# A fused attention and fp8 linear kernel: the weights prepared in the order of their use, one scale for each

## The reference

```
xn  = layernorm(x)                               # x: 8 x 2048 x 512, float32, no gain or bias
qkv = xn @ Wqkv.T + bqkv                         # 512 -> 1536
q, k, v in 16 heads of 32; attention runs over the FIRST axis (8 positions), for each of the 2048 columns
mask: rows 0-3 see keys 0-3 only (prompt groups of 4), rows 4-7 see all 8 keys
out = x + softmax(q k / sqrt(32) + mask) v @ Wproj.T + bproj
        + fp8(xn) @ fp8(Wffn).T + bffn           # the same xn; both operands rounded to fp8
```

## Time and profile before

| | |
|---|---|
| time, median of 3 | 1569.23 us (1569.12 to 1570.31) |
| the profiled execution | 1569.3 us, its span 1567.5 us |
| PE busy | 1506.4 us, 96% of the span, 6913 matmuls |
| DVE | 1442.0 us, 92% |
| POOL | 1378.9 us, 88% |
| ACT | 1048.3 us, 67% |
| mean granted TensorE clock | 0.982 |

### The profile page before, as it was taken

The page is one execution under the profiler, slowest core; times in us unless marked ns, Lnnn a source line. Parts: engine busy times, 40 slices in busy tenths (PEclk is TensorE's granted clock), DMA queues, the critical chain, the costliest instruction groups (busy, mean ns, idle before and its releaser), DMA issues. The chain is left out here.

```text
span 1567.5 us, 23119 instructions
## 1 busy us (share of the span) xinstructions
PE 1506.4 (96%) x6913; PEld 681.0 (43%) x6913; DVE 1442.0 (92%) x1188; ACT 1048.3 (67%) x2010; POOL 1378.9 (88%) x1046
## 2 busy tenths in 40 slices
PE   4999999999999999999999999999999999999956
PEld 3444444444444444444444444444444444444412
DVE  7389999999999999999999999999999999999992
ACT  5676667676766767666776776676776667776432
POOL 1288999899899989999998999999899999999885
PEclk8999999999999999999999999999999999999977
DMA  5334454545455454544545455454544445454322
GB/s 197 76 89 113 113 124 118 128 113 128 118 121 121 116 132 106 132 116 125 123 109 134 111 127 122 119 124 111 134 112 128 119 116 128 113 131 97 91 78 81
DMA packets 366508, 184.00 MB, mean 117 GB/s; under 512 B 314160, under 2 KB 314160, under 8 KB 366384
## 3 DMA queue, kind: packets, MB, share of 16 engines
q1 hardware_dynamic: 366384, 182.53, 47.5%
HBM read 73.41 MB, written 33.55 MB: 68 GB/s over the span
## 5 line engine op out<-in xcount | busy, mean ns | idle before, releaser
L391 POOL TENSOR_TENSOR prod_pv<-kv,probs 128x2048 f32<-128x2048 f32 x192 | 699.3, 3642 | 10.0
L758 DVE TENSOR_REDUCE o_nat<-prod_pv 128x512 f32<-128x2048 f32 (+1 forms) x128 | 429.1, 3352 | 51.7 <-POOL prod_pv L391 34.9
L725 DVE TENSOR_REDUCE scores<-prod_qk 128x64 f32<-128x2048 f32 x192 | 439.3, 2288 | 6.6
L720 DVE TENSOR_TENSOR prod_qk<-q_ps,kv 128x1536 f32<-128x1536 f32 (+1 forms) x192 | 397.8, 2072 | 2.2 <-ACT kv L557 2.2
L602 PE MATMUL proj_ps<-wproj_hi,oT 128*128 128x512 f16 x1032 | 339.2, 390 | 0.0
L602 PE MATMUL k_ps<-wqkv_hi,xT 128*128 128x512 f16 x1024 | 327.0, 381 | 5.4 <-DMA xT<-x 5.1
L602 PE MATMUL v_ps<-wqkv_hi,xT 128*128 128x512 f16 x1024 | 325.4, 379 | 0.0
L602 PE MATMUL q_ps<-wqkv_hi,xT 128*128 128x512 f16 x1024 | 325.4, 379 | 0.0
L566 ACT ACTIVATE kv<-v_ps 128x512 f32<-128x512 f32 x128 | 142.3, 1112 | 156.3 <-PE v_ps L602 156.2
L602 PE MATMUL proj_ps<-wproj_lo,oT 128*128 128x512 f16 x516 | 202.1, 392 | 0.0
L602 PE MATMUL k_ps<-wqkv_lo,xT 128*128 128x512 f16 x512 | 195.1, 381 | 0.0
(11 more groups left out here) (117 smaller groups left out, 1853.4 us busy)
## 6 DMA issues: line engine op xcount, KB each, us to landing
xn<-in_L_attn_x SPq DMA_DIRECT2D x128, 256.0 KB, 2.8
xs<-in_L_attn_x SPq DMA_DIRECT2D x128, 256.0 KB, 2.6
out<-xs SPq DMA_DIRECT2D x128, 256.0 KB, 2.1
xT<-x SPq DMA_TRANSPOSE x256, 3.0
kv<-in_L_attn_Wqkv SPq DMA_DIRECT2D x3, 1024.0 KB, 10.4
oT<-o SPq DMA_TRANSPOSE x128, 3.2
kv<-in_L_ffn_weight SPq DMA_DIRECT2D x1, 1024.0 KB, 5.6
kv<-in_L_attn_Wproj SPq DMA_DIRECT2D x1, 1024.0 KB, 14.3
```

What stands on the lines that cost most here:

```text
L391: nc.gpsimd.tensor_tensor(o, v, p, ALU.mult).then_inc(pv_multiplied, 1)
L720: nc.vector.tensor_tensor(prod_qk[:, 1:1 + m0 + 4 - m1, :], qb, k, ALU.mult).then_inc(qk_multiplied, 1)
L725: nc.vector.tensor_reduce(scores[:, n % 2, :, m0:m0 + 4].rearrange("p h m -> p m h"), prod_qk[:, row:row + 4, :].rearrange("p m (h d) -> p ...
L758: nc.vector.tensor_reduce(o_nat[:, n % 2, :], prod_pv[:, place:place + units, :].rearrange("p q (c m) -> p c q m", m=4), AX_XY, ALU.add).t ...
```

## The change

Every weight gets a scale of its own (keys, values, queries, projection, in this order), so that the keys' can be used before the others are loaded. On POOL there are four `partition_all_reduce` of one column in place of one of two columns. SP loads two tiles of x first, then the keys' weight, and the fp8 weight last. The prologue's steps are moved into the slots of each engine. The weights' natural copies move to other parts of `kv`, `prod_pv` and `prod_qk`, since they live longer. Cut to its core:

```diff
 SP, ahead of the slots
-load Wffn; load keys', values', queries' weight; load Wproj; bqkv; k_bias; q_bias; v_bias; bproj; bffn
+            load_x(0, 0)
+            load_x(0, 1)
+            sp.dma_start(wqk_nat[:, 0:KC], ...)            # keys
+            ... bqkv; load_x(0, 2); values; k_bias; queries; q_bias; load_x(0, 3)
+            ... Wproj; v_bias; bproj; bffn; Wffn
 POOL
+            def largest(what):
+                pool.wait_ge(amax_parts, what + 1)
+                nc.gpsimd.partition_all_reduce(amax[:, what:what + 1], amax_part[:, what:what + 1], P, ...)
             def slot(i, j):
-                if at(i, j, L_SOFT):
+                if at(i, j, L_KV):
+                    largest(KEYS)
+                    scale_bias(k_bias, bk_loaded, KEYS, k_bias_ready)
+                    largest(VALUES)
+                if at(i, j, L_KV + 1):
+                    largest(QUERIES)
+                    scale_bias(q_bias, bq_loaded, QUERIES, q_bias_ready)
+                if at(i, j, 7):
+                    largest(PROJ)
+                if at(i, j, 9):
+                    scale_out_biases()
+                if at(i, j, 11):
                     pool.wait_ge(out_bias_summed, 1)
                     split_into_rows(bo_all, out_bias_rows)
+                    pool.wait_ge(small_ready, 2)
+                if at(i, j, 13):
+                    pool.wait_ge(wffn_transposed, KC)
 ACT (high_parts now waits for scales_ready of its weight)
+ slot 4, first: high_parts(0, 4); before the keys' copy: preset_k(), high_parts(4, 8);
+                before the values' copy: high_parts(8, 12)
+ slot 5: the three diagonals; preset_q(0) waits for q_bias_ready
+ slots 7, 8: high_parts(12, 14), (14, 16); 9, 10: q_small, q_half_small; 12, 13: keep_wffn
 PE
+            turn_parts(0, 2 * KC + 2)                       # 10 parts ahead of the slots
+ slot 4: wait for w_ready 4, open k_ps; keys of tile 0; turn_parts(10, 12); wait for w_ready 8,
+         open q_ps 0 and 1; values of tile 0
+ slot 5: wait for w_ready 12 before queries; slot 6: open q_ps 2 and 3
+ slots 7, 8: turn_parts(12, 14), (14, 16)
+ slot 10: the values' bias projected (slot 5 before); slots 11, 12: turn_wffn (24 matmuls each)
+ slot 14: open proj_ps
 DVE
+                if at(i, j, 3):
+                    largest_of_rows(KEYS)
+                if at(i, j, 4):
+                    scale_of(KEYS)
+                    largest_of_rows(VALUES)
+                    low_parts(0, KC)
+                if at(i, j, 5):
+                    scale_of(VALUES)
+                    largest_of_rows(QUERIES)
+                    low_parts(KC, 2 * KC)
+                    scale_of(QUERIES)
+                    low_parts(2 * KC, 3 * KC)
+                if at(i, j, 6):
+                    largest_of_rows(PROJ)
+ slot 7: scale_of(PROJ), low_parts(12, 14), clip and halve Wffn; 8: low_parts(14, 16)
+ slot 9: split the values' bias; slot 10: wait for its projection, add the output biases
```

## The result

The changed kernel takes 1591.88 us (median of four runs, 1590.62 to 1592.41) against 1569.31 for the kernel before on the same chip: 1.0142 times as long, 95% interval 1.0129 to 1.0154. The run profiled took 1592.07 us with a span of 1590.3, against 1567.5: the spans differ by 22.8 us, the medians by 22.6.

A forecast was written before the change was run, and what follows sets the result against it. PE's stream was taken to set the time from the first key product, with DVE a second limit from 100 to 160 us; 1569.3 + 18.3 (DVE's lateness) = 1587.6, said as 1588 us; range 1565 to 1597, the forecast's own 1580 to 1597.

The forecast's parts named there:

- The price of the reductions: On POOL, four reductions between ordinary instructions mean eight changes of code, each taken at 6.5 or 7.03 us.
- the unseen change *into* a reduction: On POOL, code must also be brought in ahead of a reduction; bounds 0 and 7.03 us, hidden before by an 18.05 us wait.
- the first pair: POOL's changes into and out of the keys' reduction, taken at 7.03 us each; the weights' loads may have stretched the one seen.
- the six later ones: POOL's changes of code around the values', queries' and projection's reductions, estimated at 6.5 us each.
- D: Rival: all eight changes at 7.03 us or more, PE at low clock after gaps: 1591 to 1597; chance 0.70 together with the forecast.
- Tile 0's keys: On PE, the first key products start at 25.9 us, 13.4 us earlier; transposes land no earlier than about 25.9.
- The wait in slot 10: DVE waits some 5 us for the projected values' bias before tile 2's scores; 15.9 us from PE's slot 10 to tile 4.
- this chain alone decides: DVE's chain reaches tile 4's slot at 114.3 us against 96.01, 18.3 us late, and sets the end.
- POOL's split of the bias in slot 11: POOL's 6.4 us split moves to slot 11, leaving tile 8's transposes about 4 us early; counted at nothing.
- Rival A: The change of code into the reduction, or the later changes, are free on POOL: 2.3 us won, 1567 us; chance 0.14.
- B: Rival: POOL's changes of code at half the price, 3.6 us each: about 1576 us; chance 0.10.
- C: Rival: as Rival A, and the transposes overtake the weights; keys of tile 0 at 20, 1561 us; chance 0.06.

The follow-up runs named there:

- e1: Changed kernel with each of POOL's four partition reductions replaced by a copy of the one column, the maximum over partitions left out: 1568.28 us, ratio 0.9996.
- e9: Changed kernel with the last-needed loads (projection's and fp8 weight, values' and output biases) issued behind tile 1's transposes: 1590.27 us, ratio 1.0138.
- e4: Changed kernel with DVE's wait for the values' bias and its addition moved to the end of slot 10, behind tile 2's scores: 1590.59 us, ratio 1.014.
- e10: e5 and e9 together, with the queries' maximum transposed only behind tile 0's keys so the keys' bank opens early: 1565.62 us, ratio 0.9979.
- e5: Changed kernel with the maxima made exactly by DVE and a PE transpose, not POOL's reductions; queries' scale and some weight parts reordered: 1570.21 us, ratio 1.0008.
- e11: e10 with DVE's addition of the output biases moved behind tile 2's scores, as in e4: 1564.67 us, ratio 0.9975.
- e2: Changed kernel with all four maxima in DVE's slot 3 and one POOL reduction of four columns in slot 4: 1573.7 us, ratio 1.0031.
- e3: Kernel before with one more POOL partition reduction at the head of slot 7, its result unused: 1576.76 us, ratio 1.005.
- e7: Changed kernel, POOL's four reductions kept, with the last-needed loads issued behind tile 0's transposes: 1592.5 us, ratio 1.0147.
- e6: e5 with the last-needed loads (projection's and fp8 weight, biases) issued behind tile 0's transposes, not ahead of them: 1570.28 us, ratio 1.001.

## Why the prediction was right, and where it was off

**The price of the reductions** was the forecast's whole case, and it holds: e1 takes them away and 23.6 us with them. The forecast's 1588 is 3.9 us short of the 1591.9 measured. The guess that the unseen change *into* a reduction also costs something, with nothing in the trace but a wait in front of it, is right: 5.85 to 8.71 us. The Trainium skill (GPSIMD Engine Reference, "2.1 Instruction dispatch") gives 5.95 us for first-called code; the trace agrees for the three later ways in (5.85 to 6.02, beside DMA shares of 0 to 0.44), while the first took 8.71, and the three later ways out 6.9 to 7.5 us.

**The mis-sized term is the first pair.** I took 7.03 us for each and argued that the change seen before might have been *stretched* by the weights' loads. It was the other way round: in the kernel before it fell late in the loads (a DMA share of 0.31 from 20.8 to 27.8 us), and the early order puts the first pair into their middle: 8.71 and 11.66, 6.3 us more than taken, less 0.7 because POOL was free earlier than I had it (9.21 against 9.9). For the six later ones I took 39.0 us in all; they took 39.1. That it fits so well is in part luck: the ways in were under the 6.5 I took for each, the ways out above it. Everything behind the first pair is late by about the same amount, 5.0 to 5.6 us: the keys of tile 0 at 31.4 (forecast 25.9), low part of tile 1 at 45.7 (40.2), of tile 2 at 64.4 (58.9), of tile 4 at 85.2 (79.6), keys of tile 4 at 88.5 (82.9), slot 10 at 104.0 (98.4), tile 4 on DVE at 119.3 (114.3). With DVE's measured 23.3 us in the place of 18.3 the sum is 1592.6; measured 1591.9. So the time lies where D had it (1591 to 1597), though not by D's terms: five of the eight changes were under 7.03 us, and from tile 4's keys to 1500 us there was low clock only in the keys at 190.30, where it fell after three matmuls.

**Tile 0's keys** I bounded by the transposes, at 25.9. They waited for ACT's preset with the keys' bias, and that for POOL: 29.95 + 0.68, then 30.67 to 31.27. The bound itself was too low. The transpose into `xT` was issued at 19.25 and landed 9.7 us later, at about 28.95, 3 us after my 25.9 and 2.5 ahead of the keys. In e1, where POOL is out of the way, it landed at 27.45 and the keys waited 8.72 us for it, to 27.51. So with the pair at my price the keys of tile 0 would have started at some 27.5 to 29 us (an estimate from these two landings). It cost nothing further on, since tile 1's low part hangs on POOL and not on these keys. In e9, with the later loads away, the keys stand at 26.0 with POOL's change again in front.

**The wait in slot 10** was 5.55 us, forecast about 5, and from PE's slot 10 to tile 4 on DVE it took 15.3 us, forecast 15.9. That this chain alone decides is refuted by e4. What I had put at nothing, POOL's split of the bias in slot 11, is the second chain of the same length: with the values' bias in slot 10, both the addition and the split fall where no slack is.

**Rival A** failed at its premise, but e1, which makes its premise true, has its number on DVE to the digit (93.7) and its time within 1.3 us: a start 12 to 13 us earlier is mostly lost in what is put between the later slots. **B**, 3.6 us a change, fails on the same rows: none took under 5.85. **C**, the transposes ahead of the weights, wasn't tried alone. In e10 tile 0's transpose landed at 19.3, near the 20 that C took for the keys, but the keys waited for their bank until 24.37, and the time was 1565.6 against C's 1561.

## What to carry to other kernels

Read an idle time in front of a POOL instruction whose releaser is only "issue" as a possible change of code, and count both directions: the first may be hidden by a wait in the kernel before, and becomes visible once the data come earlier. Gather such instructions into one, placed behind a wait longer than the change and where no bulk load runs, or do the step on other engines (a widened column, one transpose and a row maximum gave the same value here 3.3 us after the column, 11.57 to 14.91 in e10). And when an early start is won, ask at once which later point takes it back: 9 to 17 us won at the first product (e5, e1, e10, e11) were worth -1 to 4 at the end.

## What the runs showed of the hardware

- What stands ahead of a reduction (read here as the change of code) is done during a wait for a semaphore: in e2 the reduction started 0.22 us after its data, in e4 3.0 us after them with 6.67 us since POOL's last instruction.
- Out of the reduction it is longer beside other transfers: 6.78 to 7.45 us at a DMA share of 0 to 0.14 (after, e3, e4, e7, e9), 7.03 at 0.31 (before), 7.64 at 0.40 (e2), 9.59 at 0.70 (e9), 10.88 at 0.82 (e7), 11.66 at 1.09 (after).
- Into the reduction the link is weaker: 5.81 to 6.44 us at 0 to 0.49, 5.97 at 0.76 (e9), 6.67 (e4) to 8.71 (after) at 1.03 to 1.09. The 2 us between these two at the same share of 1.05 are not explained.
- SP takes longer to issue behind bulk loads: the first two rows below (kernel after, SP, start, duration) hold it for 8.3 us, beside a DMA share of 1.08 and 1.49, where the same two instructions took 1.18 us at a share of 0.38 and 1.23 at 0.02. Whether the queue was full isn't shown.

```profile
16.31 2.75 SPq L341 DMA_TRANSPOSE xT<-x  x1
19.25 5.50 SPq L347 DMA_TRANSPOSE xT<-x  x1
...
25.55 1.18 SPq L341 DMA_TRANSPOSE xT<-x  x1
45.81 1.23 SPq L347 DMA_TRANSPOSE xT<-x  x1
```

- After a gap in front of a key product the clock fell in some runs and not in others, and the gap's length alone doesn't tell. Behind 3.54, 3.75 and 5.76 us the matmuls ran at 1.2 GHz at once (e7, e9, e3). Behind 2.65 us they did so at once in e10 and not at all in e6. The clock fell after two matmuls behind 3.23 and after three behind 2.09 us (both after), and not at all behind 2.11 (e11), 2.40 (e1) and 2.50 (e2).
